# Two runs of transposes in a step, and cache pages copied by SyncE

## The reference

```
q, k, v = x @ Wq.T, x @ Wk.T, x @ Wv.T        # 32 query heads, 8 key/value heads, D = 128
q, k = rope(rmsnorm(q) * qw, pos), rope(rmsnorm(k) * kw, pos)
kc = k_cache[block_table].reshape(8, 512, 8, 128)      # 16 pages of 32 tokens a sequence
vc = v_cache[block_table].reshape(8, 512, 8, 128)
k_all, v_all = concat([kc, k]), concat([vc, v])        # 640 keys
probs = softmax(where(valid, q @ k_all.T / sqrt(D), -1e30))
x = x + (probs @ v_all) @ Wo.T
logits = x @ Wr.T + 5 * onehot(language)               # 8 experts, the best 2 by softmax
x = x + x @ W.T + 2 * sum_e gate_e * (x @ A_e.T) @ B_e.T
```

## Time and profile before

| | |
|---|---|
| median of 3 runs | 1166.06 us |
| the profiled execution | 1164.94 us, span 1163.1 us |
| granted TensorE clock | 0.997 |
| TensorE busy | 1144.9 us, 98% |
| VectorE, ScalarE, GpSimd busy | 918.5, 931.8, 768.7 us |
| DMA | 98.12 MB, mean 84 GB/s |

### The profile page before, as it was taken

How to read it: one execution, slowest core, us unless ns; L and a number is a source line. 1 busy time by engine, 2 the same in 40 slices (tenths; PEclk the granted TensorE clock), 3 DMA queues, 4 the chain that set the end, 5 groups by cost and what they waited for, 6 DMA issues and landing times.

```text
span 1163.1 us, 20954 instructions
## 1 busy us (share of the span) xinstructions
PE 1144.9 (98%) x6932; PEld 1025.0 (88%) x6932; DVE 918.5 (79%) x1884; ACT 931.8 (80%) x1832; POOL 768.7 (66%) x833
## 2 busy tenths in 40 slices
PE   7899999999999999999999999999999999999998
PEld 6788888889989989988998998899899899889887
DVE  7988888787788778778778877877877787787746
ACT  6888888888888888888888888888888888887741
POOL 5766766767776676776677677677766767766600
PEclk9899999999999999999999999999999999999999
DMA  7423332223222223222322222222232222221001
GB/s 235 158 74 100 122 104 84 64 87 88 77 79 92 81 68 91 89 68 87 91 78 73 91 89 64 87 89 73 82 91 81 67 89 88 64 78 56 19 1 73
DMA packets 56763, 98.12 MB, mean 84 GB/s; under 512 B 8784, under 2 KB 29136, under 8 KB 56528
## 3 DMA queue, kind: packets, MB, share of 16 engines
q1 hardware_dynamic: 44368, 63.21, 17.2%
q0 software_dynamic: 12288, 33.57, 10.1%
HBM read 90.45 MB, written 6.29 MB: 83 GB/s over the span
## 4 chain that ended last, share of the span: by engine, by line
PE 92%; DVE 3%; ACT 2%; issue 1%; DMA 0%; POOL 0%; SPq 0%; ACTq 0%; DVEq 0%; POOLq 0%
PE ps_w L306 19%; PE ps_w L308 18%; PE ps_w L307 18%; PE ps_s L1297 18%; PE ps_w L1306 9%; PE ps_w L1375 2%; PE ps_w L1273 2%; PE ps_w L1280 2%; PE ps_s L1214 1%; ACT ps L645 1%; PE ps_w L1246 1%; DVE m L868 0%; DVE w_lo L792 0%; DVE pt_lo L792 0%; DMA w_raw<-wqkv 0%
## 5 line engine op out<-in xcount | busy, mean ns | idle before, releaser
L466 POOL DMA_INDIRECT kv_raw<-kv,rows x256 | 255.6, 999 | 95.7 <-issue 62.2
L651 ACT ACTIVATE ps<-ps,recip 128x640 f32<-128x640 f32 x256 | 213.1, 832 | 64.0 <-DVE recip L902 64.0
L792 DVE TENSOR_TENSOR pt_lo<-ps_w,pt_hi 128x512 fp32r<-128x512 f32 x322 | 210.3, 686 | 67.7 <-ACT pt_hi L656 65.3
L645 ACT ACTIVATE ps<-ps,negmax 128x640 f32<-128x640 f32 x256 | 211.6, 827 | 38.9 <-DVE negmax L895 38.9
L895 DVE CUSTOM_DVE_ANT_0 ps<-ps_s,mask 128x640 f32<-128x640 f32 x256 | 210.3, 822 | 7.5 <-PE ps_s L1297 3.5
L656 ACT ACTIVATE pt_hi<-ps_w 128x512 fp32r<-128x512 f32 x256 | 152.7, 596 | 57.2 <-PE ps_w L1306 57.2
L306 PE MATMUL ps_w<-w_hi,xt_hi 128*128 128x512 f32 (+1 forms) x496 | 177.0, 357 | 1.6 <-DVE w_lo L792 1.4
L308 PE MATMUL ps_w<-w_hi,xt_lo 128*128 128x512 f32 (+1 forms) x496 | 167.1, 337 | 0.0
L307 PE MATMUL ps_w<-w_lo,xt_hi 128*128 128x512 f32 (+1 forms) x496 | 166.7, 336 | 0.0
L1306 PE MATMUL ps_w<-cst,ps 128*128 128x128 f32 x1024 | 154.1, 273 | 1.0 <-DVE w_lo L792 0.8
L484 POOL TENSOR_TENSOR rot<-u,cos 128x640 f32<-128x640 f32 x63 | 100.5, 1596 | 69.4 <-DVE u L940 69.4
(11 more groups left out here) (182 smaller groups left out, 2598.6 us busy)
## 6 DMA issues: line engine op xcount, KB each, us to landing
xt_hi<-xsplit SPq DMA_DIRECT2D x56, 256.0 KB, 2.8
xt_lo<-xsplit SPq DMA_DIRECT2D x56, 256.0 KB, 2.8
w_raw<-wqkv SPq DMA_DIRECT2D x56, 192.0 KB, 2.4
wo_raw<-wo SPq DMA_DIRECT2D x56, 128.0 KB, 2.2
kv_raw<-kv,rows POOLq DMA_INDIRECT x256, 2.9
y<-xT SPq DMA_DIRECT2D x8, 256.0 KB, 3.6
y<-x SPq DMA_DIRECT2D x8, 256.0 KB, 5.6
out<-y SPq DMA_DIRECT2D x8, 256.0 KB, 2.2
```

What stands on the lines that cost most here:

```text
L466: pool.indirect_dma_start(kv_raw[:, g % 2, t, :], None, kv[:, :], bass.IndirectOffsetOnAxis(rows[:, g % B, t:t + 1], 0)).then_inc(s_kv[g % ...
L645: nc.scalar.activation(ps[:, h, :], ps[:, h, :], ACT.Exp, bias=negmax[:, s % 2, h:h + 1], scale=-1.0, accum_out=rowsum[:, s % 2, h:h + 1]) ...
L651: nc.scalar.activation(ps[:, h, :], ps[:, h, :], ACT.Copy, scale=recip[:, s % 2, h:h + 1]).then_inc(a_norm, 1)
L792: return nc.vector.tensor_tensor(out_ap, full, hi.bitcast(F32), ALU.subtract)
```

## The change

- Order of TensorE: scores(3) goes ahead of T0, and T2 follows T1, ahead of Y; QT, KTC, KTN, T3 and TN follow each other behind Y; KV of group s+2 is last in the step. So there are two runs of transposes, of 12 and of 17. In step 0 KV comes behind T1 as before.
- Banks: `BANKS` names the uses of each bank: Q, T0, QT, KV in one; O, Y, TN; T1, KTC; T2, T3. KTN goes to columns 384 to 511 of a score bank.
- ScalarE: v_hi ahead of probs(0); probs(2) ahead of the mid-step weight split, exps(3) and norm(3); the piece of wqkv ahead of qt_hi; the piece of wo at the end. VectorE: probs(2) directly behind probs(1); the mid-step splits ahead of qt_lo; the copies for the second layer behind probs(3).
- Pages: `gather` and `gather_dma` go, with the row numbers. SyncE loads page numbers from `cin` into registers, four at a time, and issues 16 copies of a page (32 rows of 1 KB) for group s+2. At the start the pages of group 0 stand ahead of x tiles 2 and 3, and those of group 1 ahead of `keep_x(0)`.
- SyncE's waits on pe_s (two places) and pe_t go.

```diff
...
@@ -68,9 +69,8 @@
-UNITS = ["Q", "O", "T0", "T1", "Y", "T2", "QT", "KTC", "KV", "KTN", "T3", "TN"]
-NU = len(UNITS)
-NBANK = 4
+BANKS = (("Q", "T0", "QT", "KV"), ("O", "Y", "TN"), ("T1", "KTC"), ("T2", "T3"))
+NBANK = len(BANKS)
...
@@ -253,20 +251,29 @@
-            eng.wait_ge(s_kv[g % 2], 64 * (g // 2 + 1))
+            eng.wait_ge(s_kv[g % 2], 16 * NPP * (g // 2 + 1))
         def bank(unit):
-            return ps_w[:, UNITS.index(unit) % NBANK, :]
+            return ps_w[:, [unit in users for users in BANKS].index(True), :]
...
+        def new_keys_bank():
+            return ps_s[:, 1, 1, 512 - S:512]
...
+        def queries_turned_bank(g):
+            return bank("O") if g == 0 else bank("QT")
...
+        def x_turned_bank(unit):
+            return ps_s[:, 1, 1, :] if unit == "KTN" else bank(unit)
         def query_bank(g):
-            return bank("T0") if g == 1 else bank("Q")
+            return bank("T2") if g == 1 else bank("Q")
         def keys_values_bank(g):
-            return bank("O") if g == 0 else bank("KV")
+            return bank("O") if g in (0, 2) else bank("KV")
         FREES = {"O": (d_olo, 1, 1, -1), "T0": (d_pt, 5, 1, 0), "Q": (a_q, 1, 1, 2), "T1": (d_pt, 5, 2, 0),
-                 "QT": (d_qt, 1, 1, 1), "KTC": (d_ktc, 1, 1, 1), "KTN": (d_ktn, 1, 1, 1), "Y": (d_y, 1, 1, -1),
+                 "QT": (d_qt, 1, 1, 1), "KTC": (d_ktc, 1, 1, 1), "Y": (d_y, 1, 1, -1),
                  "T2": (d_pt, 5, 3, 0), "KV": (a_kv, 1, 1, 2), "T3": (d_pt, 5, 4, 0), "TN": (d_pt, 5, 5, 0)}
...
@@ -367,7 +375,6 @@
                 sp.dma_start(xt_hi[:, g % 2, :].bitcast(F32), xsplit[g % B, :, 0, :]).then_inc(s_xback[g % 2], 16)
-                sp.wait_ge(pe_s, 4 * (g - 3) + 2)
                 sp.dma_start(xt_lo[:, g % 2, :].bitcast(F32), xsplit[g % B, :, 1, :]).then_inc(s_xback[g % 2], 16)
@@ -391,6 +398,23 @@
+            def cached_pages(g):
...
+                if g == 0:
+                    sp.wait_ge(s_ints, 16)
+                wait(sp, pe_ktc, g - 2)
+                wait(sp, p_v, g - 2, 2)
+                pages = kv.rearrange("(n s) d -> n s d", s=PSIZE)
+                for part in range(PPT):
+                    at = slice(part * PSIZE, (part + 1) * PSIZE)
+                    b = I_BLOCK + g % B * CT
+                    _, ids = nc.values_load_multi_w_load_instructions(
+                        cin[part * PSIZE:part * PSIZE + 1, b:b + CT], engines=[mybir.EngineType.SP], min_val=0, max_val=PAGES - 1,
+                        skip_runtime_bounds_check_because="pages of the table are numbered from 0 to PAGES - 1")
+                    for t in range(CT):
+                        sp.dma_start(kv_raw[at, g % 2, t, :], pages[bass.ds(ids[t] + g // B * PAGES, 1)].rearrange("o s d -> (o s) d")
+                                     ).then_inc(s_kv[g % 2], 16)
@@ -406,11 +430,12 @@
             sp.dma_start(nw[:].rearrange("p h d -> p (h d)"), normw[:, :]).then_inc(s_nw, 16)
-            wait_kv(sp, 0)
+            cached_pages(0)
+            sp.dma_start(kpos_stage, kpos[:, :]).then_inc(s_kpos, 16)
             x_transposed(2)
-            sp.dma_start(kpos_stage, kpos[:, :]).then_inc(s_kpos, 16)
             x_transposed(3)
             sp.dma_start(first_wo, wo[0]).then_inc(s_wo0, 16)
+            cached_pages(1)
             keep_x(0)
@@ -418,8 +443,6 @@
                     natural_x(0)
-                if s > B:
-                    wait(sp, pe_s, s, 4, 3)
                 if s + 1 in W_MID:
@@ -429,12 +452,12 @@
                         x_transposed(c)
+                if has(s + 2):
+                    cached_pages(s + 2)
                 if HB <= s + 3 < B:
...
                     natural_x(1)
-                if s > B:
-                    wait(sp, pe_t, s, 4, 2)
                 if s + 1 in WO_MID:
@@ -451,21 +474,6 @@
-            def gather(g):
...
-                pool.wait_ge(d_rows, 1)
-                nc.gpsimd.tensor_scalar(rows[:, g % B, :], rows[:, g % B, :], float(PAGES * PSIZE), None,
-                                        ALU.add).then_inc(p_rows, 1)
...
-            def gather_dma(g):
-                wait(pool, p_rows, g)
-                wait(pool, pe_ktc, g - 2)
-                wait(pool, p_v, g - 2, 2)
-                for t in range(CT):
-                    pool.indirect_dma_start(kv_raw[:, g % 2, t, :], None, kv[:, :],
-                                            bass.IndirectOffsetOnAxis(rows[:, g % B, t:t + 1], 0)
-                                            ).then_inc(s_kv[g % 2], 16)
@@ -507,19 +515,10 @@
                     nc.gpsimd.tensor_tensor(v_lo[:, CT, :], new, v_hi[:, CT, :].bitcast(F32), ALU.subtract).then_inc(p_v, 1)
-                    if has(s + 2):
-                        gather(s + 2)
-                        gather_dma(s + 2)
...
-            pool.wait_ge(d_rows, 1)
-            for g in range(2):
-                gather(g)
-            pool.wait_ge(s_w0kv[1], 16)
-            gather_dma(0)
...
             nc.gpsimd.tensor_tensor(rstd[:], meansq[:], mhalf[:], ALU.pow).then_inc(p_rstd, 1)
-            gather_dma(1)
             pool.wait_ge(s_nw, 16)
...
@@ -657,7 +656,8 @@
                 if has(g1) and s > 0:
-                    keys_values(g1)
+                    if s > 1:
+                        keys_values(g1)
                     squares(g1)
@@ -686,15 +686,15 @@
                 if has(s):
-                    probs(0)
...
                     nc.scalar.activation(v_hi[:, CT, :], raw[:, s % 2, QW + D:WW], ACT.Copy).then_inc(a_vhi, 1)
-                if has(s):
+                    probs(0)
                     probs(1)
+                    probs(2)
                     if s in W_MID:
@@ -703,23 +703,22 @@
                     first_wo_split(0)
-                if has(s):
-                    probs(2)
+                for n in W_AT.get(s, ()):
+                    w_split(n)
                 if has(g1):
...
                     cached_keys(g1)
-                for n in W_AT.get(s, ()):
-                    w_split(n)
-                if has(g1):
                     new_keys(g1)
-                for n in WO_AT.get(s, ()):
-                    wo_split(n)
-                for unit in ("QT", "KTC", "KV", "KTN"):
+                if s == 0:
+                    keys_values(g2)
+                for unit in ("QT", "KTC", "KTN"):
                     turn_x(s, unit)
...
                     nc.scalar.activation(pt_hi[:, CT, :, :].rearrange("p h q -> p (h q)"), bank("TN"), ACT.Copy).then_inc(a_pt, 1)
+                for n in WO_AT.get(s, ()):
+                    wo_split(n)
                 if s == 0:
...
@@ -977,31 +977,27 @@
                     split_x(3)
-                if has(s):
-                    probs(2)
-                if has(g1):
-                    turned_queries(g1)
-                    cached_keys(g1)
-                if s == 0:
                     first_wo_split(0)
...
                 if has(g1):
+                    turned_queries(g1)
+                    cached_keys(g1)
                     new_keys(g1)
+                for unit in ("QT", "KTC", "KTN"):
+                    turn_x(s, unit)
+                if has(s):
+                    probs(3)
+                    wait(dve, a_pt, s, 5)
+                    low(pt_lo[:, CT, :, :].rearrange("p h q -> p (h q)"), bank("TN"),
+                        pt_hi[:, CT, :, :].rearrange("p h q -> p (h q)")).then_inc(d_pt, 1)
                 if s == G - 2:
...
                     add_half(s - (G - 2), 1)
-                for unit in ("QT", "KTC", "KTN"):
-                    turn_x(s, unit)
-                if has(s):
-                    probs(3)
-                    wait(dve, a_pt, s, 5)
-                    low(pt_lo[:, CT, :, :].rearrange("p h q -> p (h q)"), bank("TN"),
-                        pt_hi[:, CT, :, :].rearrange("p h q -> p (h q)")).then_inc(d_pt, 1)
                 if s == B:
...
@@ -1239,23 +1235,17 @@
             def turn_new_keys(g):
-                if g == 0:
-                    wait(pe, a_kv, 0)
-                else:
-                    wait_bank(pe, g - 1, "KTN")
-                nc.tensor.transpose(bank("KTN")[:, 0:S], rot[:, REP, :], ident).then_inc(pe_ktn, 1)
...
-            def project_keys_values(g, new_keys_of=None):
+                nc.tensor.transpose(new_keys_bank(), rot[:, REP, :], ident).then_inc(pe_ktn, 1)
...
+            def project_keys_values(g):
                 if g == 1:
                     wait(pe, a_q, 0)
-                elif g >= 2:
+                elif g > 2:
                     wait_bank(pe, g - 2, "KV")
...
                         pe.wait_ge(d_wlo, k // 2 + 1)
-                    if new_keys_of is not None and k == KC - 1:
-                        turn_new_keys(new_keys_of)
...
@@ -1301,6 +1290,8 @@
                     wait(pe, a_norm, s, 4, h + 1)
+                    if s == 0 and h == 2:
+                        wait(pe, a_q, 1)
                     wait_bank(pe, s, f"T{h}")
@@ -1331,15 +1322,16 @@
```

(32 more changed lines are left out.)

50 lines of the change are left out of this document (23 added, 27 removed).

## The result

The changed kernel takes 1175.74 us (median of 4 runs, 1174.57 to 1177.15), the kernel before beside it 1166.05 (4 runs, 1165.09 to 1166.17): a ratio of 1.0083, 95% interval 1.0067 to 1.0099. So it is slower by 0.8%, where +1.4% (1182 us) was forecast. The profiled execution took 1177.15 us around a span of 1175.3, 12.2 more than the span before; the medians are 9.7 apart, since the profiled execution is the slowest of its four.

A forecast was written before the change was run, and what follows sets the result against it. TensorE, busy 98% of the span, was taken as the bound. Terms -1.7 (fewer transpose runs), +12.5 (KV's wait), +1 (early steps) and +4 (start) sum to +15.8 on the 1166.06 us median: 1182 us, range 1161 to 1215.

The forecast's parts named there:

- The wait at KV: At the step's end, KV waits for qt_lo to free QT's bank: 0.24 us a steady step, +12.5 us.
- Two runs of transposes: On TensorE, two transpose runs a step instead of five save 0.01 us per run dropped: -1.7 us in all.
- The start: SyncE's group 0 pages land 2 us late for KTC(0), and step 0 loses the same again: +4 us (0 to 12).
- The early steps: Nine steps before 199.30 us: a second weight split adds to KV's wait, waits on kt_lo go: +1 us.
- The pages hidden: SyncE's 16 page copies, 0.65 us each, take 10.4 us of 15.3 available, so steady steps lose nothing.
- rival 2: ScalarE is late at qt_hi, a wait of 0.5 to 0.8 us in 61 steps: 1199 to 1218 us; chance 0.13.
- rival 3: SyncE bounds the step above 0.96 us a page: 1200 to 1300 us slightly over, about 1446 at 1.24; chance 0.13.
- rival 4: 17 transposes in a row lower TensorE's clock to half pace, 1.8 us a step: about 1278 us; chance 0.02.
- rival 1: At KV, TensorE doesn't wait for QT's bank: 1160 to 1168 us, 1163 likeliest; chance 0.20.
- the switches: TensorE's changes between matmuls and transposes, 0.01 us a run, three runs fewer a step: -1.7 us.

The follow-up runs named there:

- The corner version: Changed kernel with transposed queries in four free score-bank corners and KTN first in its run, in KV's bank: 1160.00 us, ratio 0.9949 to the kernel before (chip A).
- the order alone: Changed kernel's order and banks, but GpSimd's gathers and SyncE's waits as before: 1178.21 us, ratio 1.0103 to the kernel before (chip A).
- the pages alone: Kernel before with SyncE's page copies for GpSimd's gathers, without SyncE's waits on pe_s and pe_t: 1166.21 us, ratio 1.0005 (chip A); 0.9802 (chip C).
- the dose: Changed kernel with one more ScalarE copy of 512 columns, read by nobody, ahead of qt_hi: 1190.91 us in one run (chip B).

## Why the prediction was right, and where it was off

- **The wait at KV: right, in place, mechanism and size.** Forecast 2.01 us from QT to KV against 1.78 of stream, 0.24 a step; measured 2.01, and 0.244 a step. Forecast +12.5 us over 52 steps; measured 12.5 over the 51 that can be counted. Each of the four links that the forecast took from rows of other waits came within 0.01 us (with them KV could start at 573.04, where the forecast writes 573.05). Removing it alone returned all of it, and lengthening the chain by 0.24 lengthened the step by 0.23.
- **Two runs of transposes: too large, by most of its 1.7 us.** The 0.01 a run was the difference of two sums of rounded rows (0.97 and 0.96), and 3 x 0.01 x 62 is 1.9 and not 1.7. A third run of transposes changes the step from 17.053 to 17.047, and three runs fewer than before are worth 0.00 to 0.02 us a step. The lower bound given, 0, was the value to take.
- **The start: wrong, +4 forecast.** Two sizes were off. A page costs 0.56 at the start and not 0.65, and lands after 1.7 us and not 2.9, since 2.9 was the landing of a gather of four times the bytes. So the last page of group 0 is issued by 16.45, where the forecast had 17.4, and was there at 17.86 (the median landing would give 18.15), where the forecast had 20.3. The cached keys' transposes didn't wait, and the first scores came 0.6 us sooner than before.
- **The early steps: +1 forecast.** Between the first scores and the pair of step 10 the changed kernel loses 1.7 us (178.66 against 176.95), the sum of waits at KV that were forecast and waits on kt_lo that went. The corner version parts the two: it has no wait at KV and needs 175.12 from its first scores (21.91) to the same pair (197.03). So the waits at KV are about +3.5 here and the rest of the change -1.8, as far as the different clocks of these executions before 60 us allow that. From the start on it is +1.1, against +5 for start and early steps together.
- **The tail: 1.4 us faster, not foreseen.** It comes with the order: the order alone has it, the queries in corners too (1.9), and the pages alone don't. What in the order gives it wasn't looked into.
- **The pages hidden: right.** 9.3 to 10.1 us a step against a forecast of 10.4, and on chip A no effect on the step in either order. The rule of the Trainium skill that speaks for coalescing (DMA: Bandwidth & Descriptors, Rules for kernel authors) holds for SyncE's time, which two half pages double, but a queue with 5 us to spare doesn't pay for it. The estimate from that page's `tensor_load` figure, 9.3 us, lies between the 9.0 and 10.1 of the rows.
- **The rivals.** ScalarE late at qt_hi (rival 2) had 0.27 us to spare, against 0.1 in the forecast; the dose shows what it costs when that is gone. SyncE as the bound (rival 3) is shown at 32 copies and absent at 16. A lower clock from 17 transposes in a row (rival 4) isn't there: the steady steps run under full clock and transposes 0.11 apart. No wait at KV (rival 1) is what the version with the corners does, at 1160.0, the lower end of the 1160 to 1168 that rival was given.
- **What the prediction didn't have at all** is that the kernel before depends on the chip. It said that GpSimd isn't on the chain, so that its gathers cost nothing. That holds for the trace that was read; on chip C their removal alone is worth 24 us, through signals of TensorE that come late beside gathers, which no row of that trace shows.

Put together with the terms as measured: +12.5 for KV (what the switches gave, if anything, is in it), +1.1 for start and early steps, -1.4 for the tail, 12.2 us. The forecast of +15.8 was too high by 3.6, and it would have been 5.3 without the 1.7 of the switches, which erred the other way: that part is luck. The other 2.5 us between 1182 and 1175.74 come from comparing a median with one execution: before, the profiled execution was 1.1 below the median, after, it is 1.4 above.

## What to carry to other kernels

When an instruction is moved to stand behind the producer of its buffer's last user, add up the chain that frees the buffer (transpose, ScalarE, VectorE, semaphore) and compare it with the stream between the two, to a tenth of a microsecond: on an engine that is 98% busy the difference is the change of the step. Before giving up the order, look for other space for the one slow user; here four unused corners of banks gave it all back. And when an engine off the critical path has little slack in front of the bound (o_lo ahead of Y, 0.1 us), its time is only as stable as the things that can delay it: measure such a kernel on more than one chip. A wait that a view puts down to issue need not be one without a cause; compare the start with the end of what the instruction reads.

## What the hardware showed beyond that

- **Beside gathers issued by GpSimd, TensorE's semaphore updates can come late, on some chips.** On chip C 178 of 1052 were 0.1 to 1.9 us late, on chip B 116 and 138, and none on chip A, in the first trace of the kernel before, or without gathers. What waits for them starts late: VectorE's row maxima 23.3 us in 30 waits where the first trace has 3.5 in 8, ScalarE's copy behind TN 15.2 in 54 where it has 0.3 in one. The gathers themselves take the same on C, 997 and 999 ns.
- **Copies of 32 KB with addresses from registers** cost SyncE 0.56 to 0.63 us each with their share of four loads of four numbers, where plain issues cost 0.41 to 0.43. Without the loads it is 0.49 to 0.54 from one to the next, with 32 KB as with 16. They land in 1.7 us.
- **The clock in the first 60 us** differs from execution to execution. Granted clock is the last figure but two of these rows of stretches, first the kernel before, then the changed one:

```profile
22.00:40.00 18.00, 14.06 (x80) 12.48 (x81) 14.86 (x29) 13.30 (x28) 13.26 (x14) 0.84 0.58 197
40.00:60.00 20.00, 19.46 (x115) 17.11 (x114) 18.25 (x33) 16.91 (x34) 14.15 (x15) 0.98 0.59 191
```

```profile
22.00:40.00 18.00, 14.55 (x79) 12.65 (x79) 13.83 (x27) 12.99 (x27) 8.25 (x8) 0.80 0.56 193
40.00:60.00 20.00, 19.34 (x111) 17.45 (x110) 17.49 (x32) 16.23 (x33) 8.02 (x8) 0.92 0.55 169
```

The kernel before shows 0.81 and 0.92 on chip C, so such figures don't need the new order; whether it has a part in them is open. They may hold a part of the 1.7 us of the early steps.
